# Routing choice from differences, gates written in place, and a mixing stage without row means

## The chip, the cores and the metric

The kernel runs on one core of one Trainium2 chip. The metric is device time in microseconds (us) of one execution; each kernel is run several times, and the median counts. The engines are named as in the profile: PE (TensorE; PEld is its weight load), DVE (VectorE), ACT (ScalarE), POOL (GpSimd), and SP, which here only issues DMAs.

## The reference, cut to what matters

Two layers work on 64 x 128 tokens of 128 features. Each has a graph part and a mixture-of-experts part, all with a residual:

```
x = x + L0_gnn(layernorm(x));  x = x + L0_ffn(layernorm(x))
x = x + L1_gnn(layernorm(x));  x = x + L1_ffn(layernorm(x))

layernorm(x) = (x - mean) / sqrt(var + 1e-5)
L0_ffn: logits = flat @ router_w.T; p = softmax(logits); top 2 of 8
        g = p_top / (p1 + p2 + 1e-9);  out = sum_k g_k * expert_k(flat)
L1_gnn: agg = A_hat @ features;  h = relu(batchnorm(agg @ W1.T + b1)); ...
L1_ffn: top 2 of 8 of softmax(x @ Wr), weights divided by their sum
```

A token's two gates in layer 0, with e = exp(l2 - l1) and Z the sum of exp(l - l1) over the eight logits, are 1/(1 + e + 1e-9 Z) and e/(1 + e + 1e-9 Z). In layer 1 they are a half plus or minus half of tanh((l2 - l1)/2). The hidden batch norm of L1_gnn works on `agg @ W1.T`, where agg is a linear mix of the normalised rows; taking the mean of each row away before the mixing is the same as taking the mean over the input features away from W1.

## The kernel before, in words

There are 8192 tokens in 16 tiles of 512; a tile is four "q" of 128 tokens on the 128 partitions. Every engine has one instruction stream written out by hand, with semaphores between engines, and also between dependent instructions on one engine: `own.inc` counts an instruction's end, `dve.wait_ge(own.sem, n)` waits for it, `own.chain` does both. `beside(k)` calls in a routing function put in unrelated work (another tile's statistics) between two dependent instructions. The program's stages follow each other: the eigenvectors of the graph (0 to 288 us), layer 0's graph part with its routing (288 to about 409), layer 0's experts (to about 738), the mixing of layer 1 (to about 798), its batch norms and output product (to about 841), layer 1's routing with the shared expert beside it (to about 989), layer 1's experts.

**Routing.** Tokens are routed in 8 groups of 8 q. For each group PE makes the logits into a bank of PSUM (`logits`, L893 to L902; before a group's first tile it waits until `lg_free` says that the last group's logits are read). On DVE `choose` (L904 to L971) copies the logits to SBUF, finds the largest, marks the first expert that has it (equality, times the weights 8..1, maximum, equality again), lowers that entry by 1e30, finds and marks the second in the same way, and ends in a scan that numbers the tokens by expert (`picked`). In layer 0 it also makes the differences to the largest logit, times the row's inverse deviation `rs`; ACT's `exp` (L973) turns them into exponentials. PE's `count` (L985) turns the marks into ranks, DVE's `place` (L995) into row numbers. `gates` (L1010 to L1034) computes the gates in small tiles of 128x8, copies the first into the token's row, and a last `nop` counts up `gates` when both stand. POOL's `scatter` (L1036) sends a group's 8 q to the rows of their experts by indirect DMAs, once slots and gates are there. Each group's work is spread over steps of the loop over tiles: in layer 0 (`gnn0_*`) choose of group g is in step 2g+3, place and gates in step 2g+4, and in between DVE also adds each tile's product to the residual (L1360), takes its statistics (L1369, L1375), and every second step computes inverse roots by Newton steps (L1166 to L1179). In layer 1 (`gnn1_*`) it is the same, with the roots' steps as `beside`, and PE fills its time with the shared expert (L1925, L1932).

**Before the mixing.** PE runs `keep_warm(ps[7], 12)` (L2293, matmuls of no use, whose line is L1440) after the last expert product of layer 0. SP fetches the rows of layer 0's result tile by tile (L1744).

**Mixing** (L1747 to L1821). Per tile DVE takes four `bn_stats` (L1152) and `bn_aggr` (L1155), adds the epsilon (L1157); ACT takes the root (L1777); DVE inverts it (L1766) and makes minus mean times inverse (L1767). POOL normalises the four q (L1799, times one column, plus another); PE mixes them (L1812, 8 matmuls), ACT copies the bank (L1783), PE multiplies by W1 (L1820, 4 matmuls of 512 columns), ACT adds the bias (L1788, twice), and DVE takes the batch norm's statistics of both halves (L1760, twice), four steps behind its own step.

## Time and profile before

| what | value |
|---|---|
| median of 3 runs | 1304.44 us (1303.02 to 1304.94) |
| the profiled execution's own time | 1302.85 us |
| its span | 1301.0 us |
| PE busy | 1099.0 us, 84% of the span |
| DVE busy | 906.7 us, 70% |
| ACT busy | 575.1 us, 44% |
| POOL busy | 479.4 us, 37% |
| TensorE clock granted, mean | 0.958 of full |
| DMA moved | 182.67 MB |

The span is the time from the first to the last instruction in the profile; 1.85 us of the execution's own time lie outside it. Shares of busy time are means over stages with different limits, so a stage's own instructions have to be read for what a change in it is worth.

### The profile page before, as it was taken

To read this page: it belongs to the slowest core of one execution; us is meant where nothing else is said; L and a number is where in the kernel's file an instruction comes from. 1 tells how busy PE (TensorE), PEld (TensorE's weight loads), DVE (VectorE), ACT (ScalarE), POOL (GpSimd) and SP (SyncE) were. 2 spreads that over 40 slices of the span, in tenths; PEclk is the share of its full clock that TensorE was granted. 3 is DMA by queue.
4 is the path that set the end of the run, shared out by engine and by line. 5 is a ranking of instruction groups with operands and counts; after the bars stand their busy time and mean duration, and the time that the engine had idled before them with its cause. 6 is when DMAs were issued, how large, how long until landed. Compare 5 with 4: busy or idle time off the path is not lost.

```text
span 1301.0 us, 25242 instructions
## 1 busy us (share of the span) xinstructions
PE 1099.0 (84%) x7060; PEld 923.0 (71%) x7060; DVE 906.7 (70%) x3896; ACT 575.1 (44%) x1756; POOL 479.4 (37%) x524
## 2 busy tenths in 40 slices
PE   3555564649874999999999999799889999999995
PEld 3555553637653888978889754377768999899994
DVE  5777689866985666856667587869863667556683
ACT  2556843605651222212222257566644445444452
POOL 2200000001764444434444362004773555455551
PEclk9999999759986999999999999999999999999998
DMA  9999997000224344323332170001224444243327
GB/s 188 399 433 426 428 427 302 1 0 18 92 91 131 111 130 132 103 66 101 99 93 77 51 243 1 17 1 59 95 95 125 148 139 130 79 113 104 112 56 201
DMA packets 78875, 182.67 MB, mean 140 GB/s; under 512 B 11752, under 2 KB 51699, under 8 KB 75408
## 3 DMA queue, kind: packets, MB, share of 16 engines
q0 software_dynamic: 20544, 112.80, 21.9%
q1 hardware_dynamic: 58192, 68.27, 19.6%
q8 instruction: 57, 0.93, 0.3%
q14 instruction: 82, 0.67, 0.2%
HBM read 65.10 MB, written 119.08 MB: 142 GB/s over the span
## 4 chain that ended last, share of the span: by engine, by line
PE 65%; DVE 27%; issue 4%; ACT 1%; DMA 1%; POOL 1%; SPq 1%; DVEq 0%; POOLq 0%; ACTq 0%
PE bank L1706 18%; PE bank L1692 17%; PE bank L1695 7%; PE bank L199 4%; PE bank L1932 3%; PE bank L1678 2%; PE bank L1925 2%; PE bank L1859 2%; DVE work L337 2%; DVE u L334 2%; PE bank L1440 1%; DVE bnh L1760 1%; DVE u L184 1%; DVE u L175 1%; DVE u L170 1%
## 5 line engine op out<-in xcount | busy, mean ns | idle before, releaser
L1706 PE MATMUL bank<-wide,work 128*128 128x128 f32 x1512 | 216.4, 278 | 1.2 <-DVE work L1622 1.0
L1692 PE MATMUL bank<-work,wide 128*128 128x256 f32 (+3 forms) x994 | 215.0, 330 | 1.7 <-DVE work L1569 1.4
L1706 PEld LDWEIGHTS bank<-wide,work 128*128 128x128 f32 x1512 | 197.9, 191 | 10.8 <-DVE work L1622 5.7
L1052 POOL DMA_INDIRECT rows<-tokens,slot x128 | 126.0, 984 | 195.1 <-issue 124.8
L1650 ACT ACTIVATE work<-bank 128x256 f32<-128x256 f32 (+1 forms) x216 | 82.7, 383 | 256.9 <-PE bank L1695 233.9
L1692 PEld LDWEIGHTS bank<-work,wide 128*128 128x128 f32 (+1 forms) x994 | 154.1, 186 | 13.9 <-issue 1.8
L1537 POOL DMA_INDIRECT rows<-wide x100 | 104.4, 1044 | 121.3 <-DVE wide L1574 101.6
L199 PE MATMUL bank<-u 63*64 63x2 f32 (+61 forms) x496 | 73.7, 255 | 66.3 <-DVE u L184 65.2
L1622 DVE TENSOR_TENSOR work<-work,bank 128x256 f32<-128x256 f32 (+1 forms) x216 | 87.7, 416 | 40.8 <-ACT work L1650 40.4
L199 PEld LDWEIGHTS bank<-u 63*64 63x64 f32 (+61 forms) x496 | 64.4, 217 | 71.7 <-DVE u L184 70.4
L1558 DVE COPY wide<-wreg 128x1066 f32 (+1 forms) x142 | 100.4, 707 | 17.8 <-issue 13.8
L1695 PE MATMUL bank<-work,wide 128*128 128x256 f32 (+3 forms) x426 | 105.3, 329 | 0.0
L1659 ACT ACTIVATE work<-bank,wide 128x256 f32<-128x256 f32 x148 | 65.5, 475 | 72.5 <-PE bank L1692 72.5
L1569 DVE COPY work<-bank 128x256 f32<-128x256 f32 x144 | 60.4, 420 | 42.5 <-PE bank L1678 34.0
L1706 PE MATMUL bank<-u,work 128*128 128x128 f32 (+1 forms) x504 | 77.7, 278 | 0.1
L1932 PEld LDWEIGHTS bank<-wreg,work 128*128 128x128 f32 x512 | 65.6, 197 | 16.9 <-issue 9.1
L1692 PE MATMUL bank<-work,u 128*128 128x256 f32 (+1 forms) x322 | 75.3, 335 | 1.6 <-issue 1.6
L1695 PEld LDWEIGHTS bank<-work,wide 128*128 128x128 f32 (+1 forms) x426 | 69.0, 178 | 8.5
L1537 POOL DMA_INDIRECT plane<-wide x50 | 49.5, 989 | 65.6 <-DVE wide L1574 56.0
L1537 POOL DMA_INDIRECT out<-wide x50 | 53.9, 1079 | 50.3 <-DVE wide L1574 42.7
L1706 PEld LDWEIGHTS bank<-u,work 128*128 128x128 f32 (+1 forms) x504 | 68.8, 191 | 3.4 <-DVE work L1622 1.6
L1932 PE MATMUL bank<-wreg,work 128*128 128x128 f32 x512 | 70.0, 284 | 0.1
(450 smaller groups left out, 2357.3 us busy)
## 6 DMA issues: line engine op xcount, KB each, us to landing
rows<-wide POOLq DMA_DIRECT2D x20, 3432.0 KB, 109.8
wide<-rows SPq DMA_DIRECT2D x100, 260.0 KB, 2.8
wide<-rows SPq DMA_DIRECT2D x88, 130.0 KB, 2.2
wreg<-in_w SPq DMA_DIRECT2D x1, 4264.0 KB, 37.8
wreg<-in_w SPq DMA_DIRECT2D x1, 4112.0 KB, 14.5
tokens<-in_x SPq DMA_DIRECT2D x2, 2048.0 KB, 20.2
tokens<-in_xt SPq DMA_DIRECT2D x1, 4096.0 KB, 41.5
tokens<-plane SPq DMA_DIRECT2D x16, 256.0 KB, 5.1
```

Source lines behind the costliest of these rows:

```text
L199: T.matmul(out, A[0:rows, col:col + 1].to_broadcast([rows, N]), rhs, start=True, stop=True).then_inc(hp, 1)
L1052: return self.nc.gpsimd.indirect_dma_start(out=xs, out_offset=bass.IndirectOffsetOnAxis(ap=self.t["slot"][:, q:q + 1], axis=0), in_=self.t ...
L1537: nc.gpsimd.indirect_dma_start(out=out, out_offset=bass.IndirectOffsetOnAxis(ap=goal, axis=0), in_=t["xin"][j % RING][:, h, 0:width], in_o ...
L1558: V.tensor_copy(t["wst"][n % WAYS][:, 0:WB[layer]], W[:, bass.ds(expert * WB[layer], WB[layer])]).then_inc(s("w"), 1)
L1569: V.tensor_copy(t["xte"][j % 2], ps[6][:, 0:TS]).then_inc(s("xt"), 1)
L1622: V.tensor_tensor(t["hh"][c][0:w, :], t["hs"][c][0:w, :], ps[c][0:w, TS:2 * TS], ALU.mult).then_inc(s("hh"), 1)
L1650: A.activation(t["hs"][c][0:w, :], ps[c][0:w, 0:TS], ACT.Silu).then_inc(s("hs"), 1)
L1659: A.activation(t["hh"][c], ps[c][:, 0:TS], ACT.Gelu, bias=bias[0]).then_inc(s("hh"), 1)
L1692: ins = T.matmul(ps[c][0:n, to], w[:, a:a + n], x[:, to], start=True, stop=True)
L1695: ins = T.matmul(ps[c][0:n, to3], w[:, HID0 + a:HID0 + a + n], x[:, to], start=True, stop=True)
L1706: ins = T.matmul(ps[4 + j % 2][:, h * P:(h + 1) * P], t["hh"][c][0:n, h * P:(h + 1) * P], w[0:n, at + c * P:at + (c + 1) * P], start=(c == ...
L1932: ins = nc.tensor.matmul(ps[4 + 2 * (i % 2)][:, q * P:(q + 1) * P], t["sh"][c][:, q * P:(q + 1) * P], t["WS"][:, (CH1 + c) * P:(CH1 + c + ...
```

## The change

In `choose` the copy of the logits goes: the maximum is taken straight from the PSUM bank, and then the differences to it are written to SBUF in both layers; `lg_free` is counted by this subtraction. The first mark is one instruction (difference >= 0, times the weights) in place of two. The second largest is found among the differences, so that it is itself the gap, and the subtraction that made the gap goes in both layers; a new semaphore `largest` says that it stands. In layer 0 the products with `rs` go to tiles of their own. ACT's `exp` in layer 0 gets a third instruction, 1 + e (Copy with bias 1.0), with a wait for the second. `gates` in layer 0 loses the addition of one, the copy and the nop, and writes both gates where they belong. In the mixing stage row means are no longer taken away: W1 is centred once, by a matmul with ones (on PE, before `keep_warm`, behind a wait until DVE has finished the last expert tile, since it writes into that tile's bank) and one DVE instruction of 128x256. DVE's additions of epsilon and the products with the mean go; ACT adds epsilon as the root's bias, from a new column of the small inputs; POOL's instruction has one operation in place of two; and DVE no longer waits for its own results at the end of a step.

```diff
     def choose(...)
-        V.tensor_copy(lg, self.lg).then_inc(s("lg_free"), 1)
+        n = own.inc(V.tensor_reduce(c["m1"], group(self.lg), AX.X, ALU.max))
         beside(0)
+        dve.wait_ge(own.sem, n)
+        V.tensor_tensor(group(r["x"]), group(self.lg), per_q(c["m1"]), ALU.subtract).then_inc(s("lg_free"), 1)
+        beside(1)
         dve.wait_ge(s("lg_free"), self.past("lg_free", g + 1))
-        n = own.inc(V.tensor_reduce(c["m1"], group(lg), AX.X, ALU.max))
-        beside(1)
-        dve.wait_ge(own.sem, n)
-        n = own.inc(V.tensor_tensor(group(r["a"]), group(lg), per_q(c["m1"]), ALU.is_equal))
+        n = own.inc(V.scalar_tensor_tensor(out=r["b"], in0=r["x"], scalar=0.0, in1=w8, op0=ALU.is_ge, op1=ALU.mult))
         if self.layer == 0:
-            shift = own.inc(V.tensor_tensor(group(r["x"]), group(lg), per_q(c["m1"]), ALU.subtract))
-        dve.wait_ge(own.sem, n)
-        n = own.inc(V.tensor_tensor(r["b"], r["a"], w8, ALU.mult))
+            V.tensor_tensor(group(r["s"]), group(r["x"]), per_q(self.t["rs"]), ALU.mult).then_inc(s("shift"), 1)
         beside(2)
...
-        n = own.inc(V.scalar_tensor_tensor(out=r["a"], in0=r["o1"], scalar=-1e30, in1=lg, op0=ALU.mult, op1=ALU.add))
+        n = own.inc(V.scalar_tensor_tensor(out=r["a"], in0=r["o1"], scalar=-1e30, in1=r["x"], op0=ALU.mult, op1=ALU.add))
         beside(5)
         dve.wait_ge(own.sem, n)
-        n = own.inc(V.tensor_reduce(c["m2"], group(r["a"]), AX.X, ALU.max))
+        V.tensor_reduce(c["d"], group(r["a"]), AX.X, ALU.max).then_inc(s("largest"), 1)
         beside(6)
-        dve.wait_ge(own.sem, n)
+        dve.wait_ge(s("largest"), self.past("largest", g + 1))
+        n = own.inc(V.tensor_tensor(group(r["b"]), group(r["a"]), per_q(c["d"]), ALU.is_equal))
         if self.layer == 0:
-            gap = own.inc(V.tensor_tensor(c["d"], c["m2"], c["m1"], ALU.subtract))
-        else:
-            V.tensor_tensor(c["d"], c["m2"], c["m1"], ALU.subtract).then_inc(s("gap"), 1)
-        n = own.inc(V.tensor_tensor(group(r["b"]), group(r["a"]), per_q(c["m2"]), ALU.is_equal))
+            V.tensor_tensor(c["m2"], c["d"], self.t["rs"], ALU.mult).then_inc(s("gap"), 1)
...
     def exp(...)
+            act.wait_ge(s("exp"), self.past("exp", 3 * g + 2))
+            self.nc.scalar.activation(c["z"], c["e2"], ACT.Copy, bias=1.0).then_inc(s("exp"), 1)
...
     def gates(...)
-        n = own.inc(V.tensor_scalar(c["mx"], c["m2"], 1.0, None, ALU.add))
+        n = own.inc(V.reciprocal(self.t["pay"][:, qs, AT_G1], c["mx"]))
         beside(2)
         dve.wait_ge(own.sem, n)
-        n = own.inc(V.reciprocal(c["m1"], c["mx"]))
+        V.tensor_tensor(self.t["pay"][:, qs, AT_G2], self.t["pay"][:, qs, AT_G1], c["e2"], ALU.mult).then_inc(s("gates"), 1)
         beside(3)
-        dve.wait_ge(own.sem, n)
-        own.inc(V.tensor_copy(self.t["pay"][:, qs, AT_G1], c["m1"]))
-        own.chain(V.tensor_tensor(self.t["pay"][:, qs, AT_G2], c["m1"], c["e2"], ALU.mult))
-        V.nop().then_inc(s("gates"), 1)
...
     def mix_dve(...)
+    dve.wait_ge(S("m_sums"), 1)
+    V.scalar_tensor_tensor(out=t["w1g1"], in0=ps[5][:, 0:2 * P], scalar=-1.0 / D, in1=t["w1g1"], op0=ALU.mult,
+                           op1=ALU.add).then_inc(S("m_centred"), 1)
...
-    V.tensor_scalar(t["sd"][:, 0, :], t["mv"][:, :, 1], EPS, None, ALU.add).then_inc(eps_sem, 1)
...
-            own.chain(V.reciprocal(n[:, 0, :], t["sd"][:, 1, :]))
-            V.scalar_tensor_tensor(out=n[:, 1, :], in0=t["mv"][:, :, 0], scalar=-1.0, in1=n[:, 0, :], op0=ALU.mult,
-                                   op1=ALU.mult).then_inc(S("m_norm"), 1)
-            dve.wait_ge(S("m_norm"), s + 1)
+            V.reciprocal(t["norm"][s % 2][:, 0, :], t["sd"][:, 1, :]).then_inc(S("m_norm"), 1)
     def mix_act(...)
-            A.activation(t["sd"][:, 1, :], t["sd"][:, 0, :], ACT.Sqrt).then_inc(S("m_root"), 1)
+            if s >= 1:
+                act.wait_ge(S("m_norm"), s)
+            A.activation(t["sd"][:, 1, :], t["mv"][:, :, 1], ACT.Sqrt, bias=t["eps"]).then_inc(S("m_root"), 1)
     def mix_pool(...)
-                                          n[:, 1, q:q + 1], ALU.mult, ALU.add)
+                                          None, ALU.mult)
     def mix_pe(...)
+            if i == 0:
+                pe.wait_ge(S("m_centred"), 1)
     the stream of PE
             experts_pe(nc, pe, S, views[0], ps, 0)
+            pe.wait_ge(S("tile_ys"), NT)
+            nc.tensor.matmul(ps[5][:, 0:2 * P], t["ones"], t["w1g1"], start=True, stop=True).then_inc(S("m_sums"), 1)
             keep_warm(nc, t, ps[7], 12)
             mix_pe(nc, pe, S, t, ps)
```

## Rows read from the trace of the kernel before

**Rows 1.** Chain of waits, one mixing step (start us, us, what):
```profile
779.83 0.88 DVE bn L1152 x4
...
781.15 0.04 DVE sd L1157
...
781.23 1.28 DVE bnh L1760 x2
...
782.62 0.17 DVE norm L1767
782.81 0.88 DVE bn L1152 x4
```

**Rows 2.** Timeline of PE around the mixing (start us, us, instruction, [idle before]):
```profile
737.88 10.46 PE L1440 MATMUL bank<-consts 128*128 128x512 f32 x24
749.87 1.16 PE L1812 MATMUL bank<-AHB,work 128*128 128x128 f32 x8 [1.53 <-POOL work L1799]
752.03 1.97 PE L1812 MATMUL bank<-AHB,work 128*128 128x128 f32 x8 [1.00 <-POOL work L1799]
...
759.02 1.05 PE L1812 MATMUL bank<-AHB,work 128*128 128x128 f32 x8
...
761.63 1.05 PE L1812 MATMUL bank<-AHB,work 128*128 128x128 f32 x8
...
793.64 1.16 PE L1812 MATMUL bank<-AHB,work 128*128 128x128 f32 x8
```

**Rows 3.** Timeline of DVE and POOL ahead of the mixing:
```profile
738.08 0.61 DVE L1574 SCALAR_TENSOR_TENSOR wide<-bank,wide 128x128 f32<-128x128 f32 x2 [0.81 <-PE bank L1706]
...
748.07 1.74 POOL L1799 TENSOR_SCALAR work<-tokens,norm 128x128 f32<-128x128 f32 x4 [6.54 <-DVE norm L1767]
```

**Rows 4.** Window of PE (stretch, length, busy (x), granted clock, DMA share, GB/s):
```profile
752.00:754.00 2.00, 1.97 (x9) 0.55 0.97 273
```

**Rows 5.** Timeline of DVE, end of layer 0's gates (one group):
```profile
352.25 0.24 DVE L1369 BATCH_NORM_STATS2 bn<-tokens 128x6 f32<-128x128 f32 x1
...
352.78 0.38 DVE L1375 BATCH_NORM_AGGREGATE pair_mv<-bn 128x2 f32<-128x6 f32 x4
```

**Rows 6.** Timeline of POOL, first scatters of groups, both layers:
```profile
318.70 1.06 POOL L1052 DMA_INDIRECT rows<-tokens,slot  x1 [91.06 <-issue]
...
342.04 0.98 POOL L1052 DMA_INDIRECT rows<-tokens,slot  x1 [1.17 <-DVEq L1034]
...
353.64 0.98 POOL L1052 DMA_INDIRECT rows<-tokens,slot  x1 [1.17 <-DVEq L1034]
...
400.78 0.98 POOL L1052 DMA_INDIRECT rows<-tokens,slot  x1 [1.07 <-DVEq L1034]
...
913.44 0.98 POOL L1052 DMA_INDIRECT rows<-tokens,slot  x1 [0.80 <-POOL idle L1047]
...
924.65 0.98 POOL L1052 DMA_INDIRECT rows<-tokens,slot  x1 [0.80 <-POOL idle L1047]
```

**Rows 7.** Timeline of DVE, layer 1's choose (one group):
```profile
932.21 0.22 DVE L912 COPY rt<-bank 128x64 f32<-128x64 f32 x1
...
932.47 0.26 DVE L915 TENSOR_REDUCE rc<-rt 128x8 f32<-128x64 f32 x1
...
934.55 0.17 DVE L943 TENSOR_TENSOR rc<-rc 128x8 f32<-128x8 f32 x1
934.64 0.27 DVE L944 TENSOR_TENSOR rt<-rt,rc 128x64 f32<-128x64 f32 x1
```

**Rows 8.** Timeline of PE, the same group:
```profile
933.64 0.95 PE L900 MATMUL bank<-small,u 128*128 128x8 f32 x8
```

**Rows 9.** Groups of DVE instructions at 288 to 400 us (busy us, mean ns):
```profile
L1001 DVE TENSOR_TENSOR rt<-bank,rt 128x64 f32<-128x64 f32 x8 | 1.8, 224 | 6.2 <-PE bank L993 6.2
...
L922 DVE TENSOR_TENSOR rt<-rt,kroute 128x64 f32<-128x64 f32 x8 | 1.7, 213 | 0.0
```

**Rows 10.** Waits between 840 and 990 us (us in total, times, longest):
```profile
PEld bank L992 <- DVE rt L969: 12.8, 8, 2.5
```

More of the change, by code:

```diff
@@ L863, in per_q @@
     return ap.unsqueeze(2).to_broadcast([P, GQ, E8])
-ROUTED = dict(lg=TILES, lg_free=GROUPS, carried=GROUPS, rank=GROUPS, slots=2 * GROUPS, shift=GROUPS, gap=GROUPS, exp=2 * GROUPS,
+ROUTED = dict(lg=TILES, lg_free=GROUPS, carried=GROUPS, rank=GROUPS, slots=2 * GROUPS, shift=GROUPS, largest=GROUPS, gap=GROUPS, exp=3 * GROUPS,
               picked=GROUPS, gates=GROUPS, rested=GQ // TOGETHER * (GROUPS - 1) + 1, total=1, limits=1, limit_row=1, first=1)
@@ L1013, in gates @@
         qs = slice(g * GQ, (g + 1) * GQ)
-        dve.wait_ge(s("exp"), self.past("exp", (g + 1) * (2 - self.layer)))
+        dve.wait_ge(s("exp"), self.past("exp", (g + 1) * (3 - 2 * self.layer)))
         if self.layer == 1:
@@ L1754, in mix_dve @@
             dve.wait_ge(S(f"rows_{s}"), 16)
-            norm_sums(V, dve, own, t, t["X"][:, s * PAIRS:(s + 1) * PAIRS, :], S("m_var"))
+            for q in range(PAIRS):
+                n = own.inc(V.bn_stats(t["bn"][:, q, :], t["X"][:, s * PAIRS + q, :]))
+            dve.wait_ge(own.sem, n)
+            for q in range(PAIRS):
+                ins = V.bn_aggr(t["mv"][:, q, :], t["bn"][:, q, :])
+            ins.then_inc(S("m_var"), 1)
         if s >= 4:
@@ L2312, in _ @@
             experts_dve(nc, dve, own, S, views[0], ps, routes[0])
-            mix_dve(nc, dve, own, S, t)
+            mix_dve(nc, dve, own, S, t, ps)
             batch_norm_dve(nc, dve, own, S, t, 1, 2, t["bnh"], t["g1"], t["be1"], t["bn1"])
```

35 lines of the change are left out of this document (10 added, 25 removed).

## The prediction, made before the changed kernel ran

> **What bounds the kernel now.** I read the page first: PE is busy for 84% of the span, DVE for 70%. Those are means, so I took the chain of waits next, stage by stage, and then the timelines of single engines where the change touches them. Three places matter; the experts, which PE fills without a gap, are untouched and only start earlier or later.
>
> In the mixing, the chain of waits runs for nine tiles from one DVE instruction to the next. From one tile's first statistics to the next tile's, 779.83 to 782.81, are 2.98 us [rows 1]. The reader should see that no other engine stands in that list. PE could go faster: while it worked off a queue, at full clock, its steps came every 2.61 us, 759.02 to 761.63 [rows 2]. Its 16 steps had come late to start with, since it waited 1.53 and 1.00 us for POOL's first two tiles [rows 2] and then ran at a granted clock of 0.55 [rows 4], the lower of its two levels (1.2 GHz of 2.4).
>
> In layer 0's routing, DVE and PE hand each other the work in a loop over two tiles. POOL's scatters show its pace: 11.60 us from one group's first scatter to the next, 342.04 to 353.64, and 11.73 as the mean of the seven intervals from 318.70 to 400.78. POOL waits at each group for the gates (1.17 us idle) [rows 6]. Where POOL is late by itself, in layer 1, a group takes it 11.21 us, 913.44 to 924.65 [rows 6].
>
> In layer 1's routing, PE waits in each of the eight groups for the end of DVE's choose (L992 for L969: 12.8 us in all, 2.5 at most [rows 10]). From there to the first expert tile PE has fixed work, so PE's waiting is what can be saved.
>
> **Mixing, 5.5 us saved.** DVE's addition of epsilon and the wait for it go: from the last moment's issue to the statistics at 781.23 there would be 0.08 us instead of about 0.24, so 0.16 (half of it is the step from 781.15 to 781.23 [rows 1], the rest the end of L1155 that is no longer waited for). The product with the mean goes, with the waits on both sides: the inverse starts 1.2 us after 781.23, at 782.43 by the two L1760, and the next tile's statistics can follow it by 0.08 instead of coming at 782.81 [rows 1], so 0.30. DVE's step is 2.98 - 0.46 = 2.52 us, below PE's 2.61. PE becomes the bound of the stage. What DVE waits for is not late: it needs ACT's result of a PE step three steps back, and that loop (POOL's 1.74 [rows 3], PE's 2.61, ACT's and DVE's 0.7 each and the inverse, some 6.2 us over three steps) is 2.1 us per step.
>
> The start moves too. Without the two small instructions the first POOL tile starts 0.4 us earlier than 748.07 [rows 3], and the second can follow at POOL's own pace: it would end at about 751.2, not 752.0. On PE, the centring matmul waits for DVE's last expert tile, which ends at 738.69 [rows 3], takes about 0.4, and pushes the 24 warming matmuls (10.46 us from 737.88 [rows 2]) to end at about 749.6 instead of 748.3. That is just when the first tile's rows are there, so the later end costs nothing, and PE is idle for 0.7 us in place of 2.5. I expect no fall of the clock. The second PE step then starts at 751.2, the sixteenth 14 x 2.61 later, at 787.8, where it was at 793.64 [rows 2]: 5.8 saved. If the clock falls as before, the two slow steps from 752.03 to 759.02 stay, 6.99 us where 5.22 would do [rows 2], and 4.1 are saved. I take 5.5. Below: if each removed instruction gives back only half, nine steps of 2.75 and the start save 2.9. Above: 6.2, with the start 0.4 earlier still.
>
> Hidden: the centring on DVE (128x256, about 0.4 us) falls into the wait for the first rows, in which POOL idles for 6.54 us [rows 3] and DVE hardly less. ACT's new wait is for an inverse that DVE made before the statistics which ACT waits for anyway; behind it are only ACT's copies, so it costs 0. For POOL's instruction with one operation there is no row; 1.74 us for four with two operations [rows 3] leave 0.8 us to PE's 2.61, so anything from half to 1.4 times that is hidden.
>
> **Layer 0's routing, 3.0 us saved.** In gates, the addition of one stood between statistics; the copy, the product, the wait for it and the nop between the last statistics at 352.25 and the moments at 352.78 [rows 5]. Now the statistics start 0.07 earlier and the moments follow them by 0.20: 352.45, so 0.33 us per loop, and the loop takes 11.27. I count the stalls of single groups, by which 11.73 exceeds 11.60, as gone with the addition and the copy. The first group loses about 0.2, an estimate by what DVE's small instructions take (0.17 for L943 [rows 7]), for ACT's third instruction, which stands ahead of a copy that PE waits for there; in later groups ACT reaches exp before that copy is due. Choose itself gets shorter by some 0.45 us, which only the last group feels, as in the others PE comes to it later. POOL's own pace of 11.21 then caps the last interval. So the last group's first scatter: 318.6 + 6 x 11.27 + 11.21 = 397.4 against 400.78 [rows 6], 3.3 saved; I take 3.0 for stalls that stay. Bounds: if the loop stays at 11.60, 318.9 + 6 x 11.60 + 11.21 = 399.7, 1.1 saved; if POOL's pace rules throughout, 3.6. The experts' start hangs on POOL's last scatters, so all of it comes through; the table behind the gates on DVE moves forward by more.
>
> **Layer 1's routing, 2.4 us saved.** The copy goes, and the maximum starts 0.26 earlier (932.21 to 932.47); the equality and the multiplication (L918, L922) become subtraction and the combined mark, no gain; the gap's subtraction goes, 0.09 (934.55 to 934.64) [rows 7]. That is 0.35 a group, and eight groups of waiting PE [rows 10] take it: 2.8. Two instructions now read the bank. A product that reads the bank takes 224 ns and one of the same size from SBUF 213 [rows 9], so I count 0.05 a group for both: 0.30 x 8 = 2.4. Bounds: 0.8, if reading the bank costs 0.25 a group, and 2.8. The later `lg_free` (after the subtraction, some 0.8 us after 932.21, by about 933.0) is still ahead of the logits at 933.64 [rows 8]. If it were not, PE would wait at the logits for what it saves at L992. The scatters of layer 1 follow POOL's pace of 11.21 there and move forward with the first groups.
>
> The trace so speaks for reading the bank. The Trainium skill speaks against: "VectorE: DVE Perf Modes", Rules for kernel authors, would copy PSUM to SBUF first where many operations follow, and its section on the TRN2 errata gives a PSUM source 62 cycles at 0.96 GHz more, 0.065 us. By that two readings cost 0.13 a group beside a copy that paid it once, an estimate of about 0.6 us more in all than in my sum; the rows on products show a sixth of it.
>
> **Sum.** 5.5 + 3.0 + 2.4 = 10.9 us. Against the profiled execution (span 1301.0 and 1.85 around it, 1302.85) that is 1292.0. It was 1.6 below the median, 1304.44; against the median the sum gives 1293.5. All three parts low, 4.8 saved, give 1299.6; all high, 12.6, give 1291.8.
>
> **Rivals.** First, the mixing keeps a DVE or ACT bound: the statistics of the hidden half wait for ACT more often, and the step stays near 2.75. For it: DVE at 2.52 and PE at 2.61 are near each other, and ACT has four instructions a step in a fixed order. Against: the loop of 2.1. Price 2.6, so 1296.1.
>
> Second, layer 0's loop does not shorten, as PE or ACT takes up what DVE gives back. For it: POOL is only 0.4 us per group from its own pace. Against: DVE is the last before each scatter in all seven later groups. 1.1 is saved there in place of 3.0: 1295.4.
>
> Third, on the other side: the clock. PE now waits in front of the warming matmuls, 0.7 us for DVE's last tile, and starts the mixing one step nearer. If the granted clock fell there and stayed low while PE works in the stage, a step would take 5.2 us (twice 2.61), not 2.98: 2.2 more for each. With the 5.4 of the two other parts, three low steps eat the gain, and fifteen make 1304.44 + 33 - 5.4 = 1332. For it: the fall to 0.55 at 752 after 2.5 us of idling [rows 2, 4]. Against: it lasted only 4 us with PE at work, and the idling shrinks to 0.7. The Trainium skill, "TensorE: Matmul & The Clock Gate", Part 1, says that the clock follows how busy PE was; by that rule, the trace agrees, it would not stay low.
>
> Fourth, the change moves nothing, because each stage's end hangs on something that I took for early: 1304.
>
> **How the numbers follow.** Forecast, 8 to 13 us saved: 0.70. First or second rival or both, 4 to 8 saved: 0.22. No change: 0.04. Slower by the clock: 0.04. The likeliest is 1293.5. The range takes in the bounds of the costs, 1291.8 to 1299.6, and half a microsecond below for what runs differ by: 1291 to 1299.5. What a measurement of this kernel can tell from no change is 0.2%, 2.6 us: faster 0.92, same 0.04, slower 0.04.
>
> **What the changed profile would show.** PE's mixing steps 2.61 us apart without idling from the third on, and its last first-product near 788 less what layer 0 saved; if they stay over 2.8 with DVE in the chain, the first rival is right. A granted clock of 1.00 from 750 to 760 (shifted): if 0.55, the start is wrong. First scatters in layer 0 about 11.3 us apart and the last 3 us earlier; if 11.6, the second rival. PE's waits for choose in layer 1 some 2.4 us less in sum than 12.8; if as long as before, reading the bank has eaten the copy. A total over 1300 would make the prediction wrong in its main point, that DVE's small instructions are on the path in all three places.

## The result, and the profile after

| | before | changed |
|---|---|---|
| median | 1303.81 us (4 runs, 1303.02 to 1304.94) | 1290.37 us (4 runs, 1289.84 to 1291.43) |
| the profiled execution's own time | 1302.85 us | 1291.43 us |
| its span | 1301.0 us | 1289.6 us |

The ratio is 0.9901, with a 95% interval of 0.9887 to 0.9915: faster by 1%, 13.4 us between the medians and 11.4 us between the two profiled executions. The forecast was 1293.5 (1291.0 to 1299.5), so the time lies 0.6 us below the range. One execution of a later kernel (e3) took 1905.79 us at a mean granted clock of 0.605, where its other four show 0.959 to 0.967; no ratio here contains it.

Cut at the same events in both traces, the 11.4 us are distributed as follows (us). "Saved" is before less changed; the forecast stands beside it. "DVE's last tile" is the start of DVE's last product of layer 0's experts, at 738.08 and 733.17 us. These are two single traces, and a difference of half a microsecond in a row can be one of executions and not of kernels.

| stage, and the event that ends it | before | changed | saved | forecast |
|---|---|---|---|---|
| to layer 0's first scatter | 318.70 | 318.18 | 0.52 | |
| first to last group's first scatter | 82.08 | 78.67 | 3.41 | 3.0 for all of layer 0 |
| to the first expert tile (PE transposes) | 15.76 | 15.60 | 0.16 | |
| layer 0's experts, to DVE's last tile | 321.54 | 320.72 | 0.82 | 0 |
| warming and mixing, to the next warming | 59.99 | 57.03 | 2.96 | 5.5 |
| batch norms, output, layer 1's routing | 191.20 | 188.23 | 2.97 | 2.4 |
| layer 1's experts | 311.73 | 311.17 | 0.56 | 0 |

**Mixing.** The chain of waits of the changed kernel in the mixing, beside [rows 1] (start us, us, what):

```profile
773.87 1.72 PE bank L1803 x4
775.59 0.89 PE bank L1793 x8
776.48 1.72 PE bank L1803 x4
778.20 0.89 PE bank L1793 x8
```

DVE is gone from the chain. PE's two kinds of matmul fill a step, 775.59 to 778.20, which is the 2.61 us forecast. The start is different. PE's timeline, beside [rows 2], and POOL's instruction in the view of one tile (min/median/max in ns):

```profile
733.84 0.70 PE L2277 MATMUL bank<-small,consts 128*128 128x256 f32 x2 [0.70 <-DVE wide L1549]
734.38 10.46 PE L1415 MATMUL bank<-consts 128*128 128x512 f32 x24
745.23 1.16 PE L1793 MATMUL bank<-AHB,work 128*128 128x128 f32 x8 [0.39 <-POOL work L1780]
747.55 1.71 PE L1793 MATMUL bank<-AHB,work 128*128 128x128 f32 x8 [1.17 <-POOL work L1780]
749.05 3.05 PE L1803 MATMUL bank<-work,small 128*128 128x512 f32 x4
751.94 1.05 PE L1793 MATMUL bank<-AHB,work 128*128 128x128 f32 x8
```
```profile
L1780 POOL TENSOR_SCALAR work<-tokens,norm x64: 594/604/607, 742.8 to 784.8; 128x128 f32<-128x128 f32 x64
```

The same view of the kernel before, where the instruction has two operations, and then a window of the changed kernel's trace (busy time of PE, PEld, DVE, ACT and POOL, then PE's granted clock, DMA share and GB/s):

```profile
L1799 POOL TENSOR_SCALAR work<-tokens,norm x64: 444/453/462, 748.1 to 793.1; 128x128 f32<-128x128 f32 x64
```
```profile
748.00:750.00 2.00, 2.00 (x9) 1.48 (x8) 0.98 (x8) 0.59 (x1) 2.00 (x5) 0.50 1.19 297
```

The form with one operation is a third slower: four take 2.35 us, not 1.74 [rows 3]. PE starts the second tile 2.32 us behind the first and idles 1.17 us. Then its granted clock falls to 0.50, as it fell before the change (0.55 in [rows 4]), and the step from 747.55 to 751.94 takes 4.39 us instead of 2.61.

**Layer 0's routing.** DVE at the end of a group's gates, beside [rows 5]:

```profile
339.36 0.15 DVE L1020 TENSOR_TENSOR tokens<-tokens,rc 128x8 f32<-128x8 f32 x1
339.43 0.28 DVE L1344 BATCH_NORM_STATS2 bn<-tokens 128x6 f32<-128x128 f32 x1
339.63 0.36 DVE L1350 BATCH_NORM_AGGREGATE pair_mv<-bn 128x2 f32<-128x6 f32 x4
```

The moments follow the last statistics by 0.20 us, where they took 0.53. POOL's first scatters of groups, beside [rows 6]:

```profile
351.98 0.97 POOL L1039 DMA_INDIRECT rows<-tokens,slot  x1 [0.80 <-POOL idle L1034]
...
363.20 0.97 POOL L1039 DMA_INDIRECT rows<-tokens,slot  x1 [0.80 <-POOL idle L1034]
...
396.85 0.97 POOL L1039 DMA_INDIRECT rows<-tokens,slot  x1 [0.80 <-POOL idle L1034]
```

The releaser is now POOL's own clearing instruction, as it was in layer 1 before. The first two groups are 11.40 us apart, all others 11.19 to 11.22. That is POOL's own pace in this trace. It differs between executions: in the traces of e1, e3, e5, e9 and e12 POOL is also its own releaser, but a scatter takes 1.00 to 1.01 us in the mean instead of 0.98, and the groups are 11.4 us apart.

**Layer 1's routing.** PE's wait for choose, beside [rows 10], and DVE's groups of the first two instructions of choose (busy us, mean ns):

```profile
PEld bank L984 <- DVE rt L959: 9.6, 8, 2.0
```
```profile
L915 DVE TENSOR_TENSOR rt<-bank,rc 128x64 f32<-128x64 f32 x8 | 2.2, 273 | 0.0
...
L912 DVE TENSOR_REDUCE rc<-bank 128x8 f32<-128x64 f32 x8 | 1.7, 218 | 1.5 <-PE bank L900 1.5
```

The wait is 3.2 us less in sum. In the kernel before, L915 is the same reduce reading SBUF, and L918 an equality with the same operands and shape as the subtraction; its groups by line are:

```profile
L918 DVE TENSOR_TENSOR rt<-rt,rc 128x64 f32<-128x64 f32 x8 | 2.2, 273 | 0.0
L915 DVE TENSOR_REDUCE rc<-rt 128x8 f32<-128x64 f32 x8 | 2.1, 266 | 0.0
```

Reading the bank costs the 128x64 tensor operation nothing (273 and 273 ns; the subtraction itself takes 273 ns from SBUF in e10), and the reduce takes 48 ns less from the bank.

### The profile page after: what moved, and what is told of

Its sections match the earlier page's. It is cut to its first block, busy times and chain, and to the rows that moved or that the text cites. A ratio compares the mean times of both kernels' runs of the same rounds, so it can differ in the third digit from the quotient of the medians.

```text
span 1289.6 us, 25159 instructions
## 1 busy us (share of the span) xinstructions
PE 1093.8 (85%) x7062; PEld 921.5 (71%) x7062; DVE 891.7 (69%) x3809; ACT 580.3 (45%) x1764; POOL 488.2 (38%) x524
## 4 chain that ended last, share of the span: by engine, by line
PE 69%; DVE 23%; issue 3%; ACT 2%; DMA 1%; POOL 1%; SPq 1%; DVEq 0%; POOLq 0%; ACTq 0%
PE bank L1681 18%; PE bank L1667 17%; PE bank L1670 7%; PE bank L199 4%; PE bank L1915 3%; PE bank L1653 2%; PE bank L1908 2%; PE bank L1803 2%; PE bank L1842 2%; DVE work L337 2%; DVE u L334 2%; PE bank L1415 1%; DVE u L184 1%; DVE u L175 1%; DVE u L170 1%
```

## The experiments

All were run in five rounds beside the kernel before. Its medians were 1301.95 us (15 runs) beside e1 to e4, 1302.0 (19) beside e5 to e8, and 1302.52 (9) beside e9 to e12; these are about 2 us below the 1303.81 of the first comparison. "Mixing" is the stage of the table above that begins with DVE's last expert tile.

**e1, routing part alone.** The change's edits in choose, exp and gates; the mixing as before. A part of its edit against the changed kernel:

```diff
 def mix_pe(...):          # and mix_dve, mix_act, POOL's product: as before
-            if i == 0:
-                pe.wait_ge(S("m_centred"), 1)
```

> The kernel before with the routing part alone (choose, exp and gates in both layers); the mixing stage is as before. Theory: the routing part gives about 7.5 us of the profiled 11.4: layer 0 about 4 (POOL's scatters of groups 11.2 us apart throughout), layer 1 about 3 (PE waits for choose about 9.6 us in all instead of 12.8), time about 1296.3; the mixing steps stay 2.98 us apart. Rival: the routing's gain is worth only what I forecast, 5.4 us together, and the rest of the change's 13 us comes from the mixing: 1298.4. A third: its gain depends on the mixing part as well (a common cause, such as the clock), then it is under 4 us, over 1300.

1294.66 us, ratio 0.9938 (0.9924 to 0.9951), 7.3 us between the medians. That is the theory's 7.5, and more than the 5.4 that the forecast gave to both routing parts. Its time of 1296.3 was missed because the kernel before was faster in this series than when the theory was made. Its groups in layer 0 were not 11.2 us apart but 11.4 (318.37 to 397.96 for seven). Mixing 59.89 us, as before; the span 1293.0.

**e2, mixing part alone.** Routing as before. A part of its edit against the changed kernel:

```diff
 def choose(...):          # and exp, gates: as before
-        n = own.inc(V.tensor_reduce(c["m1"], group(self.lg), AX.X, ALU.max))
+        V.tensor_copy(lg, self.lg).then_inc(s("lg_free"), 1)
```

> The kernel before with the mixing part alone (centred W1, no row means, epsilon as the root's bias, one operation on POOL); routing is as before. Theory: it gives about 3 us in the profile, not the 5.5 forecast, since POOL's instruction with one operation takes 604 ns instead of 453, its second tile comes late, PE waits 1.2 us and the granted clock falls as before; time about 1300.8, PE's steps 2.61 us apart. Rival: the mixing part is worth 5.5 us or more in most runs, and only the profiled run of the changed kernel was one with the low clock there: 1298 or less, and the profile shows a clock of 1.00 from 745 to 760 us.

1300.91 us (11 runs, 1296.71 to 1301.88), ratio 0.9986 (0.9977 to 0.9995): 1.0 us between medians, 1.8 by the ratio. The theory's 1300.8 was met by luck: it stood for 3 us saved from 1303.8, and the kernel before took 1301.95 here. Its mixing took 55.45 us, 4.5 less than before, yet the span fell only from 1301.0 to 1300.1. The layer 1 stage, where its instructions are those of before, took 194.09 us against 191.20. One window over that stage in either trace (stretch, length, then busy time of PE, PEld, DVE, ACT and POOL, then PE's granted clock, DMA share and GB/s), the kernel before first, then e2:

```profile
798.07:989.27 191.20, 171.45 (x898) 118.22 (x896) 135.17 (x624) 111.41 (x202) 66.75 (x73) 0.96 0.16 56
```
```profile
793.69:987.78 194.09, 174.44 (x897) 120.46 (x896) 134.95 (x624) 111.55 (x202) 66.56 (x73) 0.94 0.17 58
```

PE's idle time (length less busy) is 19.75 and 19.65 us. The 3.0 us are in PE's busy time with the same matmuls, at a mean clock of 0.94 instead of 0.96. This scatter is in every trace of the stage:

| stage before layer 1's experts | length | PE busy | PE idle | clock |
|---|---|---|---|---|
| old choose: before, e2, e6, e11 | 191.20, 194.09, 193.17, 191.34 | 171.45, 174.44, 172.75, 171.14 | 19.75, 19.65, 20.42, 20.20 | 0.96, 0.94, 0.95, 0.96 |
| new choose: changed, e1, e7, e8, e12 | 188.23, 187.62, 189.04, 189.30, 186.77 | 171.68, 171.17, 172.59, 172.63, 170.01 | 16.55, 16.45, 16.45, 16.67, 16.76 | 0.95, 0.95, 0.95, 0.95, 0.96 |

The idle column separates the versions cleanly: 20.0 against 16.6 us in the mean, 3.4 us for the new choose. The busy column moves by up to 4.4 us (170.0 to 174.4) and is high where the clock is low. This places e2's loss in one execution. It doesn't explain why 11 runs have a median only 1.0 us below the kernel before, when the mixing stage alone is 4.5 us shorter; that stays open.

**e3, POOL's product with two operations.**

```diff
-                                          None, ALU.mult)
+                                          0.0, ALU.mult, ALU.add)
```

> The changed kernel with a second operation on POOL again (times the inverse, plus the constant 0.0). Theory: the number of operations sets POOL's duration: 453 ns, the second tile is ready 0.6 us or more earlier, PE's wait before it falls from 1.17 to about 0.2 to 0.6 us, and if the clock then holds, the mixing ends 2 to 3 us earlier: 1288. Rival: what makes it slow is something else (DVE's denser use of the memory beside it), then it stays near 600 ns and the time near 1290.4. Another: 453 ns need the second scalar to be a column; with a constant it is 604.

1287.56 us, ratio 0.9887 (0.9871 to 0.9902). Mixing 53.72 us; PE waits only 0.19 us for the second tile. POOL's instruction takes 376 ns, less than the theory's 453, and the constant doesn't make it slow, as the second rival had it. The repeat, e12, is read below.

**e4, longer warming.**

```diff
-            keep_warm(nc, t, ps[7], 12)
+            keep_warm(nc, t, ps[7], 14)
```

> The changed kernel with 14 warming calls before the mixing in place of 12: PE's matmuls of no use end 1.7 us later, at about the time at which POOL's second tile is ready less one tile's product. Theory: the clock falls because PE idles 0.4 and 1.2 us there; with that filled, the granted clock stays at 1.00, the slow step is gone and 1.3 to 1.8 us are saved though the first product starts later: 1289. Rival: the clock's fall does not depend on these pauses; then PE is late by up to 0.5 us and the slow stretch stays: 1290.4 to 1291.

1290.1 us, ratio 0.9905 (0.9891 to 0.9919), equal to the changed kernel. The 28 matmuls end when the first tile stands and the second nearly does: PE runs 16 mixing matmuls in 2.34 us with 0.13 us idle between the tiles. The clock stays full, and mixing takes 55.36 us. That is 1.7 us less than in the changed kernel's first trace, and no less than in its second (55.30, e8 below), where the clock stayed full without this. So the longer warming spends on useless work what the wait costs, and whether it kept the clock up is not shown by one trace.

**e5, both cures** (e3's edit and `keep_warm` with 13).

> The changed kernel with POOL's product written as two operations (constant 0.0 added, as in e3) and 13 warming calls (26 matmuls) in place of 12 ahead of the mixing. Theory: the late second POOL tile was the only thing wrong at the start, and e3 and e4 are two cures of it; together they give no more than the better one. Then PE starts the mixing at full clock with a wait under 0.3 us, the last expert tile to the end of mixing takes 53.5 to 55.4 us (e3 53.72, e4 55.36, changed kernel 57.03), and the time is that of e3, 1287.5, within 1. Rival: the two add up, since each removes its own part (POOL's pace, the clock): 1285.5. A second rival: the longer warming only delays the first step, by half of e4's 1.7 us: 1288.5.

1289.32 us, ratio 0.9897 (0.9882 to 0.9911); mixing 54.23 us. The two do not add up: 26 matmuls, no wait, full clock, but a stage half a microsecond longer than e3's, as the first mixing product starts 11.75 us behind the end of DVE's last expert tile and not 10.89. The time is that of neither theory: 0.8 over the first's upper end.

**e6, gates alone.** The kernel before with the new gates of layer 0.

```diff
+            act.wait_ge(s("exp"), self.past("exp", 3 * g + 2))
+            self.nc.scalar.activation(c["z"], c["e2"], ACT.Copy, bias=1.0).then_inc(s("exp"), 1)
 ...
-        n = own.inc(V.tensor_scalar(c["mx"], c["m2"], 1.0, None, ALU.add))
-        own.inc(V.tensor_copy(self.t["pay"][:, qs, AT_G1], c["m1"]))
-        V.nop().then_inc(s("gates"), 1)
```

> The kernel before with layer 0's gates alone as in the change (one plus the second exponential on ACT, gates written in place); choose and mixing as before. Theory: in layer 0 the gates stood last before each scatter, and with 0.33 us less per group POOL's own pace of 11.21 rules all groups: the last group's first scatter about 397.3 (before 400.78, changed kernel 396.85), layer 1 unchanged (its stage about 191), 3 us saved in all: 1299 beside 1302 of before. Rival: the loop needs the shorter choose as well, and stays at 11.5 or more: last first scatter over 399, 1 us saved. Open: whether the 0.8 us that layer 0's experts gain come with the gates or with choose.

**e7, choose alone.** The complement: new choose in both layers, gates and mixing as before. A part of its edit against the changed kernel:

```diff
 def gates(...):           # as before
-        n = own.inc(V.reciprocal(self.t["pay"][:, qs, AT_G1], c["mx"]))
+        n = own.inc(V.tensor_scalar(c["mx"], c["m2"], 1.0, None, ALU.add))
```

> The kernel before with choose alone as in the change, in both layers (no copy of the bank, differences to the maximum, no gap subtraction); gates and mixing as before. Theory: layer 0's groups keep DVE's gates as their last step and gain at most the last group's 0.4 and the 0.5 of the first; layer 1's stage gains the whole 2.4 to 3.0 forecast for choose, which PE's shorter waits at L992 show (12.8 before, about 9.6). So 3 to 3.5 us saved, 1298.5 beside 1302. Rival: shorter choose also shortens layer 0's loop, since gates wait behind it on DVE: groups 11.2 apart, 6.5 saved as in e1 (1294.7).

e6: 1300.85 us (12 runs), ratio 0.9989 (0.9978 to 1.0001), 1.9 over its forecast and not clear of no change. e7: 1298.17 us, ratio 0.9968 (0.9957 to 0.9979). POOL's waits between 330 and 400 us, e6 first (us in total, times, longest):

```profile
POOL rows L1049 <- POOL idle L1044: 5.6, 7, 0.8
```
```profile
POOL rows L1042 <- DVEq L1024: 6.9, 6, 1.2
POOL rows L1042 <- POOL idle L1037: 0.8, 1, 0.8
```

With the gates alone POOL waits for nobody else, its groups are 11.2 us apart, and the last group's first scatter is at 397.59; with choose alone DVE is the releaser six times, the groups stay 11.6 apart (the last 11.2), and it is at 399.67. So the gates alone are enough for the loop's gain, as the theory said. The choose part alone gives 1.2 of it: the two intervals of 12.0 us that the kernel before has are 11.6 here, and the last one is 0.3 shorter. In layer 1 it is the reverse: PE idles 20.42 us in e6 and 16.45 in e7. Of the 3.2 us by which e6's last group came earlier, about 1.2 is left between medians, in a scatter of 1296.7 to 1304.4. In the profiled execution its layer 1 stage had 1.3 us more PE busy time than before's, where e2's had 3.0; for the median this is as open as in e2. e7 came out at its forecast, 1298.2 beside 1298.5.

The 0.8 us in layer 0's experts are two waits that the kernel before, e6 and e7 have and that the changed kernel and e8 do not have. In the trace of before:

```profile
695.63 0.49 PE L1706 MATMUL bank<-wide,work 128*128 128x128 f32 x2 [0.35 <-DVE work L1622]
...
722.93 0.49 PE L1706 MATMUL bank<-wide,work 128*128 128x128 f32 x2 [0.37 <-DVE work L1622]
```

The stage is 320.7 to 320.9 us in e1, e3, e4, e5, e8, e9 and e12, which have both parts of the new routing and no copy. It is 321.4 to 321.7 in e2, e6, e7 and e11, and 321.25 in e10, where the copy is back; all five have the two waits. How an earlier start makes DVE just timely there stays open.

**e8, the changed kernel again.**

> The changed kernel itself, on the same chip as e5 to e7. Theory: of the 13.4 us between the medians about 11.4 belong to the change (what the two profiled executions show, 1302.85 to 1291.43), the rest to what executions differ by, mostly in layer 1's routing, where the granted clock dips differently each time: here 11 to 12 us less than before. Rival: the change is worth 13.4 and its profiled execution was a late one: 13 or more less than before here too.

1291.2 us beside 1302.0, ratio 0.991 (0.9895 to 0.9924): 10.8 us between medians, 11.7 by the ratio. That is the theory's 11 to 12. The interval reaches from 9.9 to 13.7 us, so the rival's 13 is less likely and not excluded. Its trace shows the start of the mixing with the same wait and another clock (1.00, the third value from the end of the window's line):

```profile
747.87 1.16 PE L1793 MATMUL bank<-AHB,work 128*128 128x128 f32 x8 [1.16 <-POOL work L1780]
748.87 1.88 PE L1803 MATMUL bank<-work,small 128*128 128x512 f32 x4
750.59 1.05 PE L1793 MATMUL bank<-AHB,work 128*128 128x128 f32 x8
```
```profile
748.00:750.00 2.00, 2.00 (x11) 1.44 (x12) 1.31 (x9) 0.66 (x2) 2.00 (x4) 1.00 1.19 293
```

The second tile is as late as in the first profile, but the step takes 2.72 us, not 4.39, and mixing 55.30 us. After a wait of 1.00 to 1.17 us for the second tile the clock fell in the traces of before, changed, e1, e6 and e11, and stayed in those of e2, e7, e8 and e10. So the same kernel can do either, and the fall in one trace is no property of the version. Whether the version changes how often it happens is not settled: it fell in four of five traces with the old mixing and in one of four with the new one. The mixing part is worth 3.0 us with it on both sides (59.99 to 57.03) and 3.5 without it (58.80 in e7 to 55.30).

**e9, the centring behind the warming** (on top of e3).

```diff
+            keep_warm(nc, t, ps[7], 12)
             pe.wait_ge(S("tile_ys"), NT)
             nc.tensor.matmul(ps[5][:, 0:2 * P], t["ones"], t["w1g1"], start=True, stop=True).then_inc(S("m_sums"), 1)
-            keep_warm(nc, t, ps[7], 12)
```

> e3 (POOL's product in two operations) with the centring matmul, and its wait for DVE's last expert tile, behind the 24 warming matmuls instead of ahead of them. Theory: the first mixing step waits for POOL's first tile in any case, so PE gains nothing by not waiting 0.70 us ahead of the warming; the mixing takes 53.7 us as in e3, and PE's wait for the first tile grows by what the warming ends earlier (about 0.7). Same time as e3 run beside it. Rival, from the third rival of the forecast: PE's 0.7 us of waiting ahead of the warming brings the granted clock nearer to its fall, and without it the clock stays up more surely; then the stage is shorter than e3's or its scatter less. Against both: if DVE's centring now comes between the first statistics, the second PE step is up to 0.5 late.

1294.69 us, ratio 0.9935 (0.9922 to 0.9949): 5 us slower than e12 beside it. Neither theory had it. DVE's timeline of e9 shows why, and below it PE's:

```profile
743.76 0.43 DVE L1728 SCALAR_TENSOR_TENSOR small<-bank,small 128x256 f32<-128x256 f32 x1 [10.12 <-PE bank L2278]
744.10 0.86 DVE L1734 BATCH_NORM_STATS2 bn<-tokens 128x6 f32<-128x128 f32 x4
```
```profile
743.13 0.59 PE L2278 MATMUL bank<-small,consts 128*128 128x256 f32 x2
747.50 3.78 PE L1793 MATMUL bank<-AHB,work 128*128 128x128 f32 x16 [3.78 <-POOL work L1780]
```

DVE's centring stands first in its stream, so the statistics of all tiles queued behind a matmul that now came after 10 us of useless ones. They began at 744.10, where the changed kernel has them at 740.88 with the rows just landed:

```profile
740.88 0.87 DVE L1734 BATCH_NORM_STATS2 bn<-tokens 128x6 f32<-128x128 f32 x4 [5.88 <-DMA tokens<-plane]
```

PE idled 3.78 us, the granted clock was 0.50 for the next 5 us, and mixing took 58.91 us.

**e10, the copy back in choose** (on the changed kernel).

```diff
-        n = own.inc(V.tensor_reduce(c["m1"], group(self.lg), AX.X, ALU.max))
+        V.tensor_copy(r["lg"], self.lg).then_inc(s("lg_free"), 1)
+        dve.wait_ge(s("lg_free"), self.past("lg_free", g + 1))
+        n = own.inc(V.tensor_reduce(c["m1"], group(r["lg"]), AX.X, ALU.max))
...
-        V.tensor_tensor(group(r["x"]), group(self.lg), per_q(c["m1"]), ALU.subtract).then_inc(s("lg_free"), 1)
+        n = own.inc(V.tensor_tensor(group(r["x"]), group(r["lg"]), per_q(c["m1"]), ALU.subtract))
```

> The changed kernel with the copy of the logits from the bank back in choose, maximum and subtraction reading the copy, in both layers; nothing else changed. Theory: in layer 1 PE waits in each of eight groups for the end of choose, and 0.25 to 0.35 us more on DVE per group (the copy and a reduce of 260 instead of 224 ns) comes back whole: PE's idle time in layer 1's routing rises from 16.6 to about 19 us and its waits at the counts from 9.6 to about 12 us; layer 0's groups stay at POOL's 11.2 to 11.4 us apart, since there the gates and not choose came last, and only the time after the last group gets up to 0.5 longer. 2.5 to 3 us slower than the changed kernel: 1293.5. Rival: two readings of the bank cost as much as the copy did (by 0.13 to 0.25 a group), and the kernel is within 1 us of the changed one.

1294.07 us, ratio 0.9932 (0.9919 to 0.9946), 2.9 us over e8 and 3.7 over the first measurement of the changed kernel. Its waits in layer 1's routing, and the window over the stage:

```profile
PEld bank L986 <- DVE rt L961: 11.7, 8, 2.3
```
```profile
788.70:978.52 189.82, 170.91 (x897) 117.60 (x896) 134.29 (x616) 111.00 (x202) 66.35 (x73) 0.96 0.16 55
```

PE's idle time is 18.91 us, 2.3 over the mean of 16.6, and the waits at the counts are 2.1 more: the copy's price comes back through PE's waits, 0.26 to 0.29 us a group. Layer 0's groups stay 11.2 us apart (318.01 to 396.27 for seven). Two readings of the bank do not cost what the copy did.

**e11, the one-operation form in the kernel before.** It leaves out the subtraction of the row mean.

```diff
-                                          n[:, 1, q:q + 1], ALU.mult, ALU.add)
+                                          None, ALU.mult)
```

> The kernel before with POOL's instruction alone written with one operation, as in the change (multiplication by a column, None). It leaves out the subtraction of the row mean, so that its output is not the reference's; its time is that of the form alone. Theory: the form alone is slow, whatever stands around it: about 600 ns against 453, 2.3 us for four against 1.74, so the second tile of the mixing comes 0.6 to 1.1 us later than before, while the later steps, which DVE sets at 2.98 apart, hide it: mixing stage 60.0 plus 0.6 to 1.1, total 0 to 1 us slower than before. Rival: POOL's 600 ns in the changed kernel come from DVE or DMA being busier beside it there, and here the instruction takes 453 or less.

1308.04 us, ratio 1.004 (1.0026 to 1.0054): 5.5 us slower by this form alone, where at most 1 was expected. The form's duration was as expected, but the later steps did not hide it. The tile view, then the chain of waits in one step:

```profile
L1799 POOL TENSOR_SCALAR work<-tokens,norm x64: 594/605/610, 747.3 to 795.8; 128x128 f32<-128x128 f32 x64
```
```profile
773.60 0.04 DVE sd L1157
773.63 0.16 issue
773.80 1.27 DVE bnh L1760 x2
...
776.70 0.04 DVE sd L1157
776.74 0.17 issue
776.90 1.27 DVE bnh L1760 x2
```

605 ns with the old DVE stream around it, so the form and not the company is slow. Mixing takes 63.61 us, 3.6 more. By the fourth PE step 2.0 of it are there (22.90 us after the start of DVE's last expert tile, 20.94 before), from the later tiles and a deeper fall of the clock. The rest is in the steps, 3.10 us apart instead of 2.98: between DVE's addition of epsilon (L1157) and L1760 stand 0.16 us where there were 0.04. The trace shows what that is, the addition itself, in the kernel before and in e11:

```profile
L1157 DVE TENSOR_SCALAR sd<-mv x16: 169/169/171, 747.1 to 790.1; 128x4 f32<-128x4 f32 x16
```
```profile
L1157 DVE TENSOR_SCALAR sd<-mv x16: 170/291/323, 746.4 to 792.2; 128x4 f32<-128x4 f32 x16
```

It takes 291 ns instead of 169, and those 0.12 us are on the chain. In the kernel before, the POOL instruction that runs beside the addition ends 0.11 us before it does; in e11 it ends 0.21 us after it. That POOL holds DVE up there fits this, but no run tests it by itself. The remaining 1.9 us of the difference in times are within what executions differ by.

**e12, e3 again.**

> e3 once more, beside the three others of this call. Theory: the changed kernel with POOL's product in two operations is the fastest version, 1287.5 within 1 beside a before of 1302, ratio 0.988 to 0.990; mixing stage 53.7 us; idle time of PE in layer 1's routing 16.4 to 16.8 us as in every kernel with the new choose, while what the granted clock costs there (4.5 us in e3, 6 to 8 in others) differs from one execution to the next and may be higher here. Rival: e3's first measurement was a lucky one, and it equals the changed kernel (1290).

1289.74 us, ratio 0.9901 (0.9886 to 0.9916), 1.2 over the theory's upper end and near the rival; mixing 53.87 us, PE idle 16.76 us in layer 1's stage. PE's timeline and POOL's tile:

```profile
745.15 1.05 PE L1793 MATMUL bank<-AHB,work 128*128 128x128 f32 x8
746.55 1.16 PE L1793 MATMUL bank<-AHB,work 128*128 128x128 f32 x8 [0.34 <-POOL work L1780]
747.54 1.88 PE L1803 MATMUL bank<-work,small 128*128 128x512 f32 x4
749.26 1.05 PE L1793 MATMUL bank<-AHB,work 128*128 128x128 f32 x8
```
```profile
L1780 POOL TENSOR_SCALAR work<-tokens,norm x64: 365/372/374, 743.4 to 781.4; 128x128 f32<-128x128 f32 x64
```

372 ns instead of 604, and the clock stays. The stage is 1.4 us shorter than e8's (53.87 against 55.30) and 3.2 shorter than the first profile's. Between times, the ratios 0.9887 and 0.9901 stand against the changed kernel's 0.9901 and 0.991, and the intervals overlap. Taken together, eight executions of this version have a median of 1288.3 and eight of the changed kernel one of 1291.0, but no series has both side by side. The version is the best that ran, by its traces; by its times the size of its advantage is not settled.

## Where the prediction was right, and where it was wrong

**What failed.** Two steps of the prediction failed, in opposite directions. The mixing was given 2.5 us more saving than it brought, all of it lost at its start. That alone would have made the time longer than forecast. The time fell below the range because of the other step, the lower end: the sum was tied to the median of 1304.44, which later runs of the kernel before put about 2 us too high, and only half a microsecond was left for what executions differ by. The terms for the routing, 2.5 us too low together, make up for the mixing.

**The sum was near, and not by its terms.** 10.9 us were forecast and 11.4 found between the profiled executions (1292.0 forecast, 1291.43 measured). That is partly luck, as the terms miss in both directions: mixing 2.5 too high, layer 0 1.9 too low, layer 1 0.6 too low. The 0.56 in layer 1's experts had no term either; that stage varies from 311.2 to 312.6 us between the traces.

**The mixing's start:** "For POOL's instruction with one operation there is no row; [...] anything from half to 1.4 times that is hidden." The factor was 1.35 (2.35 over 1.74 us for four), inside that bound, and in the steady steps it is indeed hidden: they are 2.61 apart. It was not hidden at the start. The paragraph on the start let the second tile follow "at POOL's own pace" with the old duration. The forecast put PE's second step 12.5 us behind the last expert tile (738.69 to 751.2); it came 13.8 behind (733.78 to 747.55), and 12.3 behind in e12 (734.26 to 746.55), where the instruction is quick. "I expect no fall of the clock" failed with it: PE idled 1.17 us at that point, and a fall followed in the first profile (1.8 us) and none in e8. With a fall the forecast had 4.1 us saved; less the 1.3 of the late tile that is 2.8, and 2.96 were measured. With the quick form 6.1 us were saved in e12 (59.99 to 53.87) and 6.3 in e3, against 5.5 to 6.2; there the instruction is even quicker than the 453 ns that the forecast reckoned with. The bound asked only whether POOL keeps up with PE and not who is waiting for the first two tiles.

**Mixing, steady state:** right. DVE is out of the chain, and PE's 2.61 rules from the third step. The first rival (a step near 2.75) did not happen in any kernel with the mixing part. The centring, its wait on PE and ACT's new wait cost nothing that the traces show where they stand; e9 shows what cover this hung on.

**Layer 0's routing:** the mechanism was right, shown by e6 against e7. The moments follow the last statistics by 0.20 us, as forecast. The forecast's own working slipped once: the statistics start 0.07 earlier and the gap after them loses 0.33, which is 0.40 a loop, and only the 0.33 went into the 11.27. With 0.40 the loop is 11.20, and that is what the changed kernel's chain shows (DVE's L1335 at 331.51 and at 342.71); as POOL's pace is 11.2 as well, the trace doesn't tell which of the two sets it. The groups saved 3.4 us in the first trace. How much is POOL's pace in that execution: by the 82.08 us of the kernel before, the ten traces with the new gates save from 2.1 to 3.8, the forecast's 3.0 among them. The 0.5 ahead of the first scatter is not shown to be a gain, since the same kernel has 318.83 in e8, as late as before. The 0.8 in the experts had no term; it comes only with both parts of the routing and without the copy (e6, e7 and e10 lack all or most of it). The second rival (1.1 saved) fell; its 399.7 is what e7, without the new gates, shows (399.67).

**Layer 1's routing:** right in mechanism, low in size. PE's waits fell by 3.2 us and its idle time by 3.4, where 2.4 were forecast. The 0.05 a group that was taken off for reading the bank should have been added: 0.35 + 0.05 a group, times 8, is 3.2. Of this, e10 puts 2.1 to 2.3 on the copy and the slower reduce; that the rest is the gap's subtraction (0.09 a group) was not run by itself. By the Trainium skill's 62 extra cycles for a PSUM source ("VectorE: DVE Perf Modes", TRN2 errata) the gain would have been about 1.8 (0.6 less than in the sum, an estimate); these traces do not show such a cost at 128x64 (273 against 273 ns, and 218 against 266).

**The parts do not add up.** By medians, routing alone saves 7.3 us (e1) and mixing alone 1.0 (e2), together 8.3 of the 10.8 to 13.4 that the change saves. Inside the routing, gates alone save 1.2 (e6) and choose alone 3.8 (e7), together 5.0 of 7.3, and the experts' 0.8 is only a part of the difference. In the profiles of e2 and e6 the missing time is PE's busy time in layer 1's stage (3.0 and 1.3 us more than before's). Why the kernels with the old choose should lose there more often is not shown by any run.

**The chances.** At the prices that it gave them, the first rival alone leaves 8.3 us saved and the second alone 9.0. Both lie in the bracket of 8 to 13 that was kept for the forecast; of the cases named beside "4 to 8", only both together (6.4 saved) lie in it.

**The third rival (the clock)** was right only in that the clock matters: it fell for one step, as it had before, and never stayed low. No change and slower were excluded by the interval.

**The range** failed by its lower end, made of the upper sum of the costs (12.6 us, 1291.8) less "half a microsecond for what runs differ by". The traces of one stage with the same instructions differ by up to 3 us of PE time (before and e2), and the 43 later runs of the kernel before give medians of 1302.0 to 1302.5, 2 us below the 1304.44 of three runs to which the sum was tied. Half a microsecond was a guess where the before-runs' own spread (1303.02 to 1304.94) showed two. From 1302.0 the same 10.9 us give 1291.1, near what the changed kernel takes (1290.37, and 1291.2 in e8). The 13.4 us of the first comparison became 10.8 in e8's; both contain the 11.4 of the traces within that scatter.

## What to carry to other kernels

An engine's slower instruction can be hidden in a loop's steady state, as in the changed kernel (steps of 2.61 us), and still set the start, where the next engine waits for the first and second tile; price it at both places. Dropping an operation from an instruction need not make it quicker (453 to 604 ns here): a row with its duration is needed, and where there is none, the start should carry the high bound. A slower instruction on one engine can also lengthen another engine's, as e11's addition shows (169 to 291 ns), and then no slack hides it. A new instruction put first in an engine's stream takes all behind it along when its input moves later. Tie a forecast to more than three runs when their spread is as wide as the margin that it leaves. Where executions scatter by the granted clock, compare PE's idle time over a stage instead of its length: it told 3.4 us apart where the lengths nearly overlapped (189.3 and 191.2).

## What the runs showed of the hardware

- POOL's tensor-scalar of 128x128: 602 to 605 ns for one operation with a column (changed kernel, e2, e11), 453 for two with two columns (before), 372 to 376 for a column and a constant 0.0 (e12, e3).
- A DVE reduce of 128x64 to 128x8: 218 ns from a PSUM bank, 266 from SBUF. A subtraction of 128x64: 273 ns from either (changed kernel, e10).
- DVE's addition of a constant on 128x4 takes 169 ns in the kernel before and 291 in e11, where the only edit is POOL's slower instruction.
- The same POOL scatters take 0.98 us in the mean in some executions and 1.01 in others, which makes a group 11.2 or 11.4 us.
- The granted clock after 1.00 to 1.17 us of PE idling ahead of the mixing's second tile fell in five of nine traces, and in both ways for one and the same kernel. In the four traces where this wait is 0.34 us or less (e3, e4, e5, e12) it stayed at 1.00; as it stayed there in three of four with the new mixing and the long wait too, four traces do not show that the shorter wait is the reason.
